# Vision tower block on one core: expert scalings moved into GpSimd's pauses, second biases read as 17 more rows of the last sums, short tile's rows read by ScalarE's queue

## The reference, cut to what matters

```
h = tokens(x)                                   # 16 images x 37 tokens = 592 tokens of 256
h = layernorm(h + attention_block(h))
logits = h @ gate_w.T; scores = softmax(logits)             # 15 experts
topk_w, topk_idx = top_k(scores, 3); topk_w /= sum(topk_w)  # -> comb[t, e]
a    = gelu(h @ fc1_g) * (h @ fc1_x + b) * geglu_mult       # per expert, F = 256
yexp = a @ fc2_w.T + fc2_b                                  # fc2_b: the second biases
y    = sum_e yexp[t, e] * comb[t, e]
ys   = shared expert of width 512, with its own second bias s_fc2_b
out  = layernorm(h + (y + ys))
```

## Time and profile before

| | |
|---|---|
| median of 3 runs | 211.78 us (211.69 to 212.29) |
| profiled execution, its own time | 211.57 us |
| its span in the profile | 209.8 us |
| TensorE busy | 199.2 us of the span |
| VectorE, ScalarE, GpSimd busy | 113.2, 94.4, 121.5 us |
| mean load of the 16 DMA engines over the span | 42.4% on SyncE's queue, 8.4% on GpSimd's |

### The profile page before, as it was taken

One profiled execution on the slowest core, in us unless ns is written; L12 is line 12 of the kernel. 1 busy time (PEld: TensorE's weight loads), 2 busy tenths in 40 slices (PEclk: granted clock), 3 DMA queues, 4 the chain that ended last, 5 costly groups with the idle time before them and its releaser, 6 DMA issues.

```text
span 209.8 us, 4431 instructions
## 1 busy us (share of the span) xinstructions
PE 199.2 (95%) x1559; PEld 124.7 (59%) x1559; DVE 113.2 (54%) x313; ACT 94.4 (45%) x219; POOL 121.5 (58%) x148
## 2 busy tenths in 40 slices
PE   7999998999998899999998999999999999999981
PEld 4776676678786675776775753355444555445630
DVE  6685697868863444264799953642344332231034
ACT  2004565477868373564557762333332433235024
POOL 0040079869989857929999877216665552347100
PEclk9999999999999999999999999999999999999996
DMA  6999999960000399922220034228985321112483
GB/s 199 391 416 314 402 415 417 425 270 0 6 3 3 97 379 376 417 83 64 78 71 22 0 100 108 78 92 304 366 326 164 92 75 53 50 50 91 145 248 116
DMA packets 13822, 38.32 MB, mean 183 GB/s; under 512 B 2697, under 2 KB 4618, under 8 KB 13802
## 3 DMA queue, kind: packets, MB, share of 16 engines
q1 hardware_dynamic: 11786, 32.54, 42.4%
q0 software_dynamic: 2016, 5.51, 8.4%
HBM read 29.27 MB, written 4.06 MB: 159 GB/s over the span
## 4 chain that ended last, share of the span: by engine, by line
PE 77%; DVE 8%; DMA 6%; issue 2%; ACT 2%; POOL 2%; SPq 1%; POOLq 0%; DVEq 0%; ACTq 0%
PE ps L383 66%; PE ps L1874 3%; PE ps L1672 2%; DMA wres<-y_dram 2%; PE ps L1914 2%; PE ps L1687 2%; DMA embed_sb<-embed 1%; POOL y_dram L668 1%; DMA embed_sb<-x_dram,gather_i 1%; DMA y_dram<-ln_mem,dest_i 1%; PE ps L1603 1%; PE ps L1530 1%; DVE over L1270 1%; POOL embed_sb L659 1%; ACT ln_mem L905 1%
## 5 line engine op out<-in xcount | busy, mean ns | idle before, releaser
L383 PE MATMUL ps<-wres,cT 128*64 (+1 forms) x360 | 63.1, 469 | 0.0
L383 PEld LDWEIGHTS ps<-wres,cT 128*64 128x64 f32 (+1 forms) x360 | 25.4, 131 | 27.7 <-issue 20.5
L668 POOL DMA_INDIRECT y_dram<-ln_mem,dest_i x21 | 20.6, 982 | 26.8 <-ACT ln_mem L875 23.4
L426 POOL TENSOR_TENSOR wres<-wres,fac_mem 128x512 f32<-128x512 f32 x22 | 27.2, 1271 | 4.3 <-DVE ln_rs L1033 4.3
L659 POOL DMA_INDIRECT embed_sb<-x_dram,gather_i x21 | 20.3, 968 | 8.2 <-issue 5.2
L1406 DVE TENSOR_TENSOR fac_mem<-ps,h 128x256 f32<-128x256 f32 x21 | 8.9, 423 | 24.0 <-ACT h L869 24.0
L869 ACT ACTIVATE h<-ps 128x256 f32<-128x256 f32 x21 | 8.0, 383 | 28.5 <-PE ps L383 28.5
L383 PE MATMUL ps<-h,stage 128*128 128x296 f32 x64 | 18.2, 422 | 0.7 <-DVE xn L1384 0.6
L1413 DVE COPY cT<-ps 128x256 f32<-128x256 f32 x21 | 8.8, 424 | 15.6 <-PE ps L383 15.6
L875 ACT ACTIVATE ln_mem<-ps 128x256 f32<-128x256 f32 x21 | 8.0, 383 | 15.8 <-PE ps L383 15.8
L383 PEld LDWEIGHTS ps<-h,stage 128*128 128x128 f32 x64 | 11.6, 190 | 5.4 <-DVE xn L1384 1.0
(11 more groups left out here) (215 smaller groups left out, 379.9 us busy)
## 6 DMA issues: line engine op xcount, KB each, us to landing
wres<-experts SPq DMA_DIRECT2D x15, 768.0 KB, 13.5
fac_mem<-experts SPq DMA_DIRECT2D x11, 256.0 KB, 8.1
wres<-ut SPq DMA_DIRECT2D x3, 768.0 KB, 8.8
embed_sb<-embed SPq DMA_DIRECT2D x5, 416.0 KB, 5.6
stage<-shared SPq DMA_DIRECT2D x2, 771.0 KB, 16.4
stage<-wres SPq DMA_DIRECT2D x2, 512.0 KB
wres<-y_dram SPq DMA_DIRECT2D x2, 512.0 KB, 4.2
wres<-y_dram SPq DMA_DIRECT2D x2, 384.0 KB, 6.3
```

The costliest lines, as they stand in the source:

```text
L383: return nc.tensor.matmul(o, w, x, start=start, stop=stop)
L426: nc.gpsimd.tensor_tensor(w1(e, c), w1(e, c), row, ALU.subtract).then_inc(less_done, 1)
L668: pool.indirect_dma_start(out=y_dram[:, :], out_offset=bass.IndirectOffsetOnAxis(ap=dest_i[:, column(i):column(i) + 1], axis=0), in_=ys[:, ...
```

## The change

It has four parts. (1) GpSimd scales experts 0 and 1 right after it has subtracted for experts 3 to 5, and experts 2 and 3 after 6 to 8; the subtraction for expert 14 and the scaling of expert 4 wait for step 11 of the routing. (2) The last tile of the expert loop is taken out of the loop: `second` of tiles 16 and 17 and their copies stand ahead of `first` of tile 20. (3) The second biases of the four full tiles are no product of their own: the mixing matrix gets 17 more rows (the weights, read from comb_dram) and yr gets 17 more rows (b2_sb, 16 times side by side), so that they are added in `whole_sums` over 113 rows. The short tile keeps its bias product. (4) The short tile's rows no longer share the reads of tiles 0 to 2: they go to columns 16 to 24 of yr by one DMA that ScalarE issues.

```diff
--- before.py
+++ after.py
@@ -84,6 +84,7 @@
 YROWS = NT * P + P * YC
 TILES_OUT = (0, 1, 4, 2, 3)
 HELD = TOPK * (NSUM - YC)
+KB = KS + NE
 
 NCOPY = NT - E
 NOVER = NTT - E
@@ -93,7 +94,8 @@
 NAR = 4
 
 ROWS_AHEAD = 4
-LESS_TO = (3, 6, 9, E)
+LESS_TO = (3, 6, 9, E - 1)
+SLOTS_END = 11
 
 MULT_POOL, MULT_MLP = 5, 7
 EARLY = 8
@@ -230,7 +232,7 @@
         g2 = sb("g2", [P, TT])
         comb = sb("comb", [P, TT, 32])
         combT = sb("combT", [P, TT, 32])
-        comb17 = sb("comb17", [NE, T])
+        comb17 = sb("comb17", [NE, LAST])
         b2_sb = sb("b2_sb", [NE, D])
         stage_mem = sb("stage", [P, NS * SHARED_COLS])
         stage = stage_mem[:, :].rearrange("p (e n) -> p e n", e=NS)
@@ -277,7 +279,8 @@
 
         mix_at = NXG * D + WC
         mix_end = mix_at + PC * (TT - 1) * SUMS
-        mix = emb_mem[0:KS, mix_at:mix_end].rearrange("p (j t s) -> p j t s", j=PC, t=TT - 1)
+        mix_rows = emb_mem[0:KB, mix_at:mix_end].rearrange("p (j t s) -> p j t s", j=PC, t=TT - 1)
+        mix = mix_rows[0:KS]
         mix_last = emb_mem[KS:P, mix_end:mix_end + PC * TOPK * SUMS].rearrange("p (j k s) -> p j k s", j=PC, k=TOPK)
         y_sums = y_dram[NT * P:YROWS, :].rearrange("(p c) d -> p c d", p=P)
         owner_at = NXG * D + TOPK * TT * P // 2
@@ -297,7 +300,7 @@
                    f1v[:, 0:W1C], xn_mem[:, 0:W1C], h0_mem[:, 0:W1C]]
         copy_w2 = [stage_mem[:, W1C:WC], h3_mem[:, W2C:2 * W2C], pt_mem[:, NXG * D + W1C:NXG * D + WC],
                    f2u_mem[:, 0:W2C], f2u_mem[:, W2C:2 * W2C], h3_mem[:, 0:W2C]]
-        yr = wres[:, 0:YC * D].rearrange("p (c d) -> p c d", c=YC)
+        yr = wres[:, 0:(YC + HELD) * D].rearrange("p (c d) -> p c d", c=YC + HELD)
 
         def w1(e, c):
             return wres[:, bass.ds(e * WC + c * 2 * F, 2 * F)]
@@ -431,17 +434,13 @@
 
         def rows_written(eng):
 
+            eng.wait_ge(y2_mm, NT)
             for j in range(NYS):
                 eng.wait_ge(st_y[j], 16 * ((NT - 1 - j) // NYS + 1))
-            eng.wait_ge(y2_mm, NT)
 
         def read_rows(eng, t):
             cols = slice(PC * t, PC * (t + 1))
-            rows = P if cols.stop <= HELD else KS
-            eng.dma_start(yr[0:rows, cols], y_sums[0:rows, cols]).then_inc(ld_y[t], 16)
-            if cols.stop < HELD < cols.stop + PC:
-                rest = slice(cols.stop, HELD)
-                eng.dma_start(yr[KS:P, rest], y_sums[KS:P, rest]).then_inc(ld_y[t], 16)
+            eng.dma_start(yr[0:KS, cols], y_sums[0:KS, cols]).then_inc(ld_y[t], 16)
 
         PROJ_BANK = (4, 5, 6, 7, 0, 1, 6, 7, 4, 5, 6, 7)
         ZB_COL = 511
@@ -532,7 +531,10 @@
                 rows = comb_dram.rearrange("e (t q c) -> e t q c", q=4, c=32)[:, :, q, :]
                 sp.dma_start(rows, combT[32 * q:32 * q + NE, :, :]).then_inc(st_comb, 16)
             sp.wait_ge(st_comb, 64)
-            sp.dma_start(comb17[:, :], comb_dram[:, 0:T]).then_inc(ld_c17, 16)
+            sp.dma_start(comb17[:, :], comb_dram[:, (TT - 1) * P:T]).then_inc(ld_c17, 16)
+            for j in range(PC):
+                sp.dma_start(mix_rows[KS:KB, j], comb_dram[:, 0:(TT - 1) * P].rearrange("e (t j s) -> e t j s", t=TT - 1, j=PC)[:, :, j]) \
+                    .then_inc(ld_c17, 16)
 
             sp.wait_ge(own_done, 1)
             all_scaled(sp)
@@ -542,7 +544,8 @@
                 sp.dma_start(copy_w1[k], wres[:, bass.ds(e * WC, W1C)]).then_inc(ld_copy, 16)
                 sp.dma_start(copy_w2[k], wres[:, bass.ds(e * WC + W1C, W2C)]).then_inc(ld_copy, 16)
 
-            sp.wait_ge(st_zero, 16)
+            sp.wait_ge(y2_mm, NT)
+            sp.dma_start(yr[KS:KB, 0:YC], b2_sb[:, :].unsqueeze(1).to_broadcast([NE, YC, D])).then_inc(ld_y[0], 16)
             rows_written(sp)
             for t in range(TT - 1):
                 read_rows(nc.sync, t)
@@ -643,14 +646,21 @@
             pool.wait_ge(ln2.out, DC)
             for e in range(LESS_TO[0], LESS_TO[1]):
                 less_first(pool, e)
+            for e in range(2):
+                expert_mult(e)
             pool.wait_ge(ln2.rs, 2)
             sums(1)
             for e in range(LESS_TO[1], LESS_TO[2]):
                 less_first(pool, e)
+            for e in range(2, 4):
+                expert_mult(e)
             pool.wait_ge(ln3.rs, 1)
             for e in range(LESS_TO[2], LESS_TO[3]):
                 less_first(pool, e)
-            for e in range(MULT_POOL):
+            pool.wait_ge(rt, SLOTS_END)
+            for e in range(LESS_TO[3], E):
+                less_first(pool, e)
+            for e in range(4, MULT_POOL):
                 expert_mult(e)
 
             def gather(i):
@@ -877,8 +887,8 @@
             tile_in(0)
             tile_in(1)
             warm(ACT.Gelu)
-            for j in range(0, NT, 2):
-                for i in range(j, min(j + 2, NT)):
+            for j in range(0, NT - 1, 2):
+                for i in range(j, j + 2):
                     gate(i)
                     if j == 0:
                         tile_in(i + 2)
@@ -887,9 +897,15 @@
                         tile_in(i)
                 for i in range(max(j - 4, 0), max(j - 2, 0)):
                     tile_out(i)
+            tile_out(NT - 5)
+            tile_out(NT - 4)
+            gate(NT - 1)
             for i in range(NT - 3, NT):
                 tile_out(i)
             warm(ACT.Sqrt)
+            act.wait_ge(st_zero, 16)
+            rows_written(act)
+            act.dma_start(yr[KS:P, YC:YC + HELD], y_sums[KS:P, 0:HELD]).then_inc(ld_y[1], 16)
 
             def last_sd(i):
                 t = TILES_OUT[i]
@@ -1288,7 +1304,7 @@
 
             def choose():
 
-                dve.wait_ge(rt, 11)
+                dve.wait_ge(rt, SLOTS_END)
                 pick_of(0, jump[:, :].rearrange("p (t e) -> p t e", t=TT))
                 dve.wait_ge(rt, 14)
                 reduce_pick(0, rt)
@@ -1449,6 +1465,9 @@
                 if j == 4 + 2 * PC:
                     for k in range(NSUM - YC):
                         mixing_last(k)
+            gated_in(NT - 3)
+            gated_in(NT - 2)
+            gated(NT - 1)
             gated_in(NT - 1)
 
             def last_norm(i):
@@ -1944,25 +1963,31 @@
                     gated_transposed(i)
                 for i in range(max(j - 4, 0), max(j - 2, 0)):
                     second(i)
+            second(NT - 5)
+            second(NT - 4)
+            gated_transposed(NT - 3)
+            gated_transposed(NT - 2)
+            first(NT - 1)
+            second(NT - 3)
             gated_transposed(NT - 1)
-            second(NT - 3)
             second(NT - 2)
             second(NT - 1)
 
-            pe.wait_ge(ld_c17, 16)
             for t in range(TT):
 
                 rows = P if t < TT - 1 else LAST
                 o = ps[0:rows, SUM_BANK[t], 0:D]
-                mm(o, comb17[:, t * P:t * P + rows], b2_sb[:, :], True, False)
+                mm(o, a_late[:, t * P:t * P + rows], stage[:, 1, W1C + D:WC], True, False)
+                if t == TT - 1:
+                    pe.wait_ge(ld_c17, 16 * (PC + 1))
+                    mm(o, comb17[:, :], b2_sb[:, :], False, False)
                 for c in range(DC):
                     mm(o[:, c * P:(c + 1) * P], hs[:, c, t * P:t * P + rows], ident, False, False)
-                mm(o, a_late[:, t * P:t * P + rows], stage[:, 1, W1C + D:WC], False, False)
             def whole_sums(t):
 
-                pe.wait_ge(ld_y[t], 32 if t == 1 else 16)
+                pe.wait_ge(ld_y[t], 32 if t < 2 else 16)
                 for j in range(PC):
-                    last = mm(ps[SUMS * j:SUMS * (j + 1), SUM_BANK[t], 0:D], mix[:, j, t], yr[0:KS, PC * t + j],
+                    last = mm(ps[SUMS * j:SUMS * (j + 1), SUM_BANK[t], 0:D], mix_rows[:, j, t], yr[0:KB, PC * t + j],
                               False, True)
                 last.then_inc(fin_mm, 1)
 
@@ -1972,7 +1997,7 @@
                     for j in range(NSUM - YC):
                         rows = SUMS if j < NSUM - YC - 1 else SUM_LAST
                         last = mm(ps[SUMS * j:SUMS * j + rows, SUM_BANK[t], 0:D], mix_last[0:rows, j, k, 0:rows],
-                                  yr[KS:KS + rows, TOPK * j + k], False, k == TOPK - 1)
+                                  yr[KS:KS + rows, YC + TOPK * j + k], False, k == TOPK - 1)
                 last.then_inc(fin_mm, 1)
 
             pe.wait_ge(mix_done, TOPK * PC + NSUM - YC)
```

## The result

Median 225.72 us (225.07 to 225.98, 4 runs) against 212.03 (211.69 to 212.75, 4 runs) for the kernel before: 1.0647 times as long, 95% interval 1.062 to 1.0674. The forecast was 222.0 with a range of 215.5 to 226. The profiled execution took 225.07 us with 223.1 of span, 13.3 more than before. One of the twelve executions of experiment 10, at 215.49 us, was of the chip's slower state and is left out of its ratio, though not of its median.

A forecast was written before the change was run, and what follows sets the result against it. TensorE was taken to bound the kernel; other work counts only where it waits, at the routing and the end. End at 220.7, less 0.5 for routing and scalings, gave 220.2 span; plus 1.8 made 222.0 us, range 215.5 to 226.

The forecast's parts named there:

- One engine for the 17 rows: Bias broadcast before the first sum: one DMA engine of 16 carries it, 13.1 us taken, lower bound 9.9.
- Rival (c): Broadcast spread over 16 engines or otherwise hidden, about 1.3 us; time 208.7, or 209.4 with 0.7 lost; chance 0.10.
- S: Start of TensorE's first sum of rows at the end: 209.3 instead of 200.16, behind broadcast and reads.
- From S to the end: Sums, norms and output: S + 9.0 at full clock, S + 12.6 at half; two thirds taken, end 220.7.
- Scatters: GpSimd's queue after the last expert products: last scatter at 192.7 instead of 193.6, 0.9 us earlier.
- Scalings: Routing and scalings together: 1.2 us won at the routing, 0.7 lost at the inverse roots, -0.5 us.
- The inverse roots: VectorE's two chains of 13 small instructions beside the moved scalings: 0.7 us lost in all.
- so they cost nothing: GpSimd's last subtraction and scaling, 4.5 us, follow the slots and end near 113, well before the gathers: no cost.
- The lock on the ports: Skill's rule: VectorE's two-SBUF-input instructions and GpSimd's SBUF reads wait for each other; part 1 would lose several us.
- the row at 109.45: VectorE instruction with two SBUF inputs beside a GpSimd scaling: 0.24 us, read as its plain time, not slowed.
- costed only as an issue: ScalarE's own read of the short tile's rows: an issue of about 0.4 us while ScalarE has nothing queued.
- The likeliest case: Case of one engine carrying the bias broadcast: time 222.0 us, slower than before; chance 0.76.

The follow-up runs named there:

- experiment 10: Kernel before with GpSimd's ten scalings ahead of the last expert's two subtractions, nothing in the pauses or held for the slots; 212.99 us, 1.0037 of the kernel before.
- experiment 1: Changed kernel with the bias broadcast issued as two transfers, 16 rows and 1 row; 217.90 us, 1.0297 of the kernel before.
- experiment 5: Changed kernel with half of the broadcast's columns in one 17-row transfer, the other half as 16 rows and 1 row; 219.36 us, 1.0357 of the kernel before.
- experiment 7: Kernel before with only part 1, the moved scalings and the held last subtraction and scaling; 212.83 us, 1.0038 of the kernel before.
- experiment 9: Kernel before with only part 2, tiles 16 and 17 finished ahead of tile 20's first product; 211.32 us, 0.9969 of the kernel before.
- experiment 4: Changed kernel without parts 3 and 4, so reads of 128 rows as before; 212.30 us, 1.0012 of the kernel before.
- experiment 12: Kernel before with part 2's tile order, the last expert's subtractions behind GpSimd's scalings, and expert 4 scaled by ScalarE; 211.14 us, 0.9962 of the kernel before.
- experiment 2: Changed kernel without part 3: biases a product again, 96 rows in the sums, nothing broadcast; 214.22 us, 1.0104 of the kernel before.
- experiment 3: Changed kernel without part 3, the short tile's read on SyncE's queue behind the second read; 213.21 us, 1.0067 of the kernel before.
- experiment 6: Changed kernel with 90 more idle matmuls ahead of the wait for the first sum; 224.90 us, 1.0619 of the kernel before.

## Why the prediction was right, point by point

- **One engine for the 17 rows (the deciding step): right.** Share 0.07 at 22 to 25 GB/s; split (experiment 1) all engines run; half of the rows give back at least 6 us (experiment 5). The Trainium skill, "DMA: Bandwidth & Descriptors", section "Why a DMA increments its semaphore by 16 and not by 1", says that a transfer uses the largest number of engines up to 16 that divides the slowest dimension of both sides. The trace agrees: 17 rows on one, 16 rows on all. Rival (c), the broadcast hidden, is out: it needed under 4 us from the issue, and the first sum had its data 18.7 us after it. Its price of 1.3 us for 272 KB over all engines was too low as well (2.6 us in experiment 1).
- **S, the first sum: 211.60 instead of 209.3.** The size was off by 2.3, and by 2.8 counting the 0.5 that the sum took off for the scalings outside of S. 0.9 is the issue (192.78 instead of 191.9), of which experiments 7 and 9 explain 0.7 by the scalings and 0.2 by the tiles' order. The other 1.4 lies in the queue of that engine, whose packets the profile doesn't show apart; which of the terms (rows, scatters, ScalarE's read, the first read) is too small stays open.
- **From S to the end: 11.5, taken 11.4, which is luck: two errors made up for each other.** I placed it between full and half clock. The clock was half throughout (0.50 from 202 on), but half clock costs less than the doubling I had used: the first sum 1.08 instead of 0.64, 42 matmuls 5.65 instead of 3.19 (experiment 4), 1.7 to 1.8 times. The last norm starts at 218.94, S + 7.3 and not S + 8.4, and 4.2 us follow, as before.
- **Scatters: the last issue 0.9 earlier was forecast, 0.49 came** (experiment 9). The landing on an engine that a transfer of another queue fills was not foreseen: 5.63 us instead of 2.42, 6.13 in experiment 5. After the change this is hidden behind the broadcast; in experiment 1 it is why the reads left late.
- **Scalings: -0.5 forecast, about +0.7 in the profile and 0.9 by the medians of experiment 7.** The routing's two slow instructions fell as forecast, with the scan behind them 1.9 us in all. The inverse roots lost 0.85 (the first, 3.26 to 4.11) and 0.5 us (the second, 3.25 to 3.74), 1.35 in place of the 0.7 taken; TensorE's waits for them rose from 1.1 to 2.2. And the last subtraction and scaling, "so they cost nothing", held up the three choices that VectorE issues at the very same step of the routing: 2.70 us for 0.83. Some 0.6 came back between these choices and the first gather, where VectorE had run beside scalings before; together +0.7. I had looked for who waits for GpSimd after the slots, not for what VectorE runs beside it. The gain was then also bounded by less than the 1.6 of waits: TensorE's wait for xn fell from 1.0 to 0.6, that for h didn't fall (0.6, then 0.7).
- **The lock on the ports that VectorE and GpSimd share, which the prediction had from the Trainium skill** ("SBUF — State Buffer", section "Who interferes with whom"), stood as a rule against this part. It is half borne out. Beside subtractions VectorE's instructions lasted to about the subtraction's end (2.70 us; in experiment 12 each engine held up the other). Beside scalings four instructions of each inverse root lost 0.15 to 0.28 us, one-input and two-input ones alike, never a whole scaling. My reading of the row at 109.45 (0.24, its plain time) as "not slowed" was one row too few: in the same trace, beside a scaling, the instruction at 111.66 took 0.48 us, and 0.16 in the changed kernel (113.04).
- **Part 4 was costed only as an issue: wrong.** It costs about 2 us without part 3 (experiments 2 and 4). After the change its reads wait on the engine of the broadcast anyway, so that it probably costs less there; that is argued, no run shows it. It is also why the expectation of experiment 2 fell short by 2 us and, with the 16 partitions and the late scatter, that of experiment 1 by 6.

By parts, in us from the ratios times 212: scalings +0.8 (experiment 7), tiles' order -0.7 (9), together +0.25 (4); part 4 +2.0 (2 less 4); part 3 +11.5 (the change less 2), of which some 2 are the half clock behind the wait (from the first sum to the end 11.5 us, 9.2 in experiment 4); the sum is the 13.7 that were measured, as it must be, since the last three terms are differences of one series of kernels; these were timed on different chips, each against the kernel before. The likeliest case came true above its centre, because most of the small terms were wrong on one side.

## What to carry to other kernels

Before a transfer is added, look at its outer row count and its partitions. 17 rows of 16 KB went over one engine, and the data behind them came 18.7 us after the issue; 16 rows went over all. Few partitions lowered the rate though the engines were busy. Such a transfer also delayed what another queue sent (a scatter landed after 5.63 us instead of 2.42). An instruction of another engine released by the same semaphore step as one of VectorE's starts beside it, so what it slows must be looked for there first. And work moved off a wait gains only until the next engine in the chain (here GpSimd for the gathers) is the one waited for.

## What the runs showed of the hardware that I had not expected

- **The partitions that a transfer reaches set the DMA rate.** 16 partitions (0 to 15 to 96 to 111; which side limits isn't told apart): 96 to 101 GB/s at share 0.84. Reads to 96 partitions, with one to the other 32: 254 to 304 GB/s at full share in experiments 2 and 3. To 128: 364 to 414. A full share is thus no sign that the engines deliver what they can. The Trainium skill, "SBUF — State Buffer", section "Door 1: The DMA port swizzle (why `[64,N]` ≈ `[32,N]`)", gives four ports of 27.2 GB/s to 16 such partitions, 109 GB/s; the trace agrees nearly. For partitions 0 to 95 its port map would put two thirds of the bytes on eight ports, at most 326 GB/s (an estimate from that page). Experiments 2 and 3 stay below; one window of experiment 5 (203 to 204), with the read to the other 32 partitions in it, has 329.
- **The fall of the clock after short waits.** Idle for 1.20 and then 0.23 us around the first sum, TensorE had half the clock from about 204.6 on (experiment 2); with one wait of 0.82 it did not (experiment 3). In experiment 2's profiled execution the fall cost 1.6 us, more than the waits. That these waits caused it isn't shown: in experiment 6 it fell during the sums, though the engine had been busy up to 2.1 us before them.
- **Issuing costs more on a loaded queue.** The four reads took SyncE 4.44 us to issue behind the 17-row transfer, 1.77 in experiment 1. It isn't so for every issue: in experiment 5 the two small transfers right behind the 17 rows took 3.52 us to issue, and the reads later on only 1.79.
